# Routed experts: up part with standing weights and pieces of 256, 320 or 384 tokens

## The reference

```python
xn = _layernorm(x, axis=-1)
s = _L0_attn_ref(xn, W1, b1, W2, b2, init_h)          # recurrence, (.., 512) -> (.., 512)
# the expert part, on x = xn reshaped to (8192, 512); E = 32, I = 1024
shared_out = _swiglu(x, shared_gate_w, shared_up_w, shared_down_w)
logits = x @ gate_w
topk_ids = jnp.argmax(logits, axis=-1)
scores = jax.nn.sigmoid(jnp.max(logits, axis=-1))[:, None]
order = jnp.argsort(topk_ids)
sorted_x = (x * scores)[order]
g = ragged_dot(sorted_x, routed_gate_w, tokens_per_expert)   # (32, 512, 1024)
u = ragged_dot(sorted_x, routed_up_w, tokens_per_expert)     # (32, 512, 1024)
d = ragged_dot(silu(g) * u, routed_down_w, tokens_per_expert)  # (32, 1024, 512)
result = x_in + s * silu(shared_out + d[argsort(order)])
```

## Time and profile before

| what | value |
|---|---|
| runs | 4072.81, 4073.63, 4076.45 us; median 4073.63 |
| profiled execution | 4077.65 us, its span 4076.0 |
| TensorE busy | 3984.7 us, 98% |
| VectorE busy | 1983.8 us, 49% |
| ScalarE busy | 2003.6 us, 49% |
| mean granted clock of TensorE | 0.991 of 2.4 GHz |
| third sweep | from about 2607 us to the end, 4076 |

### The profile page before, as it was taken

The page is one execution under the profiler, slowest core; times in us unless marked ns, Lnnn a source line. Parts: engine busy times, 40 slices in busy tenths (PEclk is TensorE's granted clock), DMA queues, the critical chain, the costliest instruction groups (busy, mean ns, idle before and its releaser), DMA issues. The chain is left out here.

```text
span 4076.0 us, 51548 instructions
## 1 busy us (share of the span) xinstructions
PE 3984.7 (98%) x17849; PEld 3230.3 (79%) x17852; DVE 1983.8 (49%) x2711; ACT 2003.6 (49%) x2512; POOL 834.1 (20%) x927
## 2 busy tenths in 40 slices
PE   7999999999989999999999999799999999999998
PEld 6888888888867888888888888588888888888886
DVE  4232323233345555555555555455656556565564
ACT  3222222222247766766676666454545455554552
POOL 2011110101014100000000000043434434444443
PEclk9999999999989999999999999899999999999999
DMA  4122121212121000110000010455657557566562
GB/s 164 65 78 77 74 80 72 82 51 90 44 81 44 32 32 31 51 42 31 31 31 31 34 59 10 151 196 190 213 173 255 196 190 258 200 229 216 191 229 87
DMA packets 197850, 447.44 MB, mean 110 GB/s; under 512 B 19737, under 2 KB 36313, under 8 KB 193954
## 3 DMA queue, kind: packets, MB, share of 16 engines
q1 hardware_dynamic: 165170, 346.24, 24.0%
q0 software_dynamic: 32624, 100.47, 7.2%
HBM read 345.90 MB, written 104.68 MB: 111 GB/s over the span
## 5 line engine op out<-in xcount | busy, mean ns | idle before, releaser
L82 PE MATMUL gate<-xT,w_hi 128*128 128x512 f32 x1536 | 601.4, 392 | 1.1 <-DVE b2all L952 1.1
L83 PE MATMUL gate<-xT,w_hi 128*128 128x512 f32 x1536 | 601.4, 392 | 0.0
L84 PE MATMUL gate<-xT,w_lo 128*128 128x512 f32 x1536 | 599.6, 390 | 0.0
L1162 DVE TENSOR_TENSOR wlo<-raw,whi 128x2048 fp32r<-128x2048 f32 x192 | 438.7, 2285 | 83.5 <-ACT whi L1158 83.5
L1367 PE MATMUL tY<-whi,thT 128*128 128x512 f32 x1264 | 426.5, 408 | 0.0
L518 DVE TENSOR_TENSOR h_act<-h_act,psU 128x512 f32<-128x512 f32 x128 | 87.9, 687 | 685.8 <-PE psU L84 685.7
L1158 ACT ACTIVATE whi<-raw 128x2048 fp32r<-128x2048 f32 x192 | 367.3, 1913 | 42.1 <-DMA raw<-in_L_ffn_routed_gate_w 17.0
L82 PEld LDWEIGHTS gate<-xT,w_hi 128*128 128x128 f32 x1536 | 288.8, 188 | 66.2 <-DVE b2all L952 2.6
L84 PEld LDWEIGHTS gate<-xT,w_lo 128*128 128x128 f32 x1536 | 289.1, 188 | 62.1
L83 PEld LDWEIGHTS gate<-xT,w_hi 128*128 128x128 f32 x1536 | 288.8, 188 | 60.2
L966 DVE SCALAR_TENSOR_TENSOR log_f<-gate,b1s,log_f 128x512 f32<-128x512 f32 x128 | 96.2, 751 | 420.4 <-ACT log_f L893 420.4
(11 more groups left out here) (187 smaller groups left out, 8454.4 us busy)
## 6 DMA issues: line engine op xcount, KB each, us to landing
raw<-in_L_ffn_routed_gate_w SPq DMA_DIRECT2D x64, 1024.0 KB, 6.5
raw<-in_L_ffn_routed_up_w SPq DMA_DIRECT2D x64, 1024.0 KB, 6.3
raw<-in_L_ffn_routed_down_w SPq DMA_DIRECT2D x64, 1024.0 KB, 6.9
xT_dram<-xT SPq DMA_DIRECT2D x16, 2048.0 KB, 6.3
xT<-xT_dram SPq DMA_DIRECT2D x14, 2048.0 KB, 7.9
x_in<-in_L_attn_x SPq DMA_DIRECT2D x16, 1024.0 KB, 5.4
xs_dram<-x_in SPq DMA_DIRECT2D x16, 1024.0 KB, 4.4
ss_dram<-y_sb SPq DMA_DIRECT2D x64, 256.0 KB, 2.1
```

The costliest lines, as they stand in the source:

```text
L82: pe.matmul(out, w[0], x[0], start=start, stop=False)
L83: pe.matmul(out, w[0], x[1], start=False, stop=False)
L84: return pe.matmul(out, w[1], x[0], start=False, stop=stop)
L1162: dve.tensor_tensor(wlo[q][:], raw[q][:], whi[q][:], ALU.subtract).then_inc(wlo_done[q], 1)
```

## The change

The third sweep works on pieces instead of tiles. An expert's tokens are cut into full pieces of 384 (`PIECE`) and a last one, whose size is rounded up to 8, 10 or 12 units of 32 tokens: 256, 320 or 384. The sort is changed to give slots in units of 32 and a `plan` for each expert: first piece, first unit, first third group, number of full pieces, units of the last piece. VectorE writes in the recurrence sweep, for each piece, its expert and its size to `listed`.

In the up part the weights stand (128 inputs by 128 hidden channels) and the tokens of the piece stream, in 256, 320 or 384 columns. There are 16 blocks (gate and up for 8 groups of 128 hidden channels) of 12 matmuls. The result has hidden channels on the partitions, as the down part wants it, so `turn_h` is gone. The down part has 24 matmuls of 512 columns for each 128 tokens, into one of three psY banks; the third group is behind a condition. TensorE runs one loop over `listed`; only its up part has a program for each size. The other engines still loop over experts, with a full-piece program and one of three for the last piece. The raw weight buffers are three in a ring instead of six; each weight part is 1 MB as before, but a part of the up weights now holds 256 channels of gate and of up. Gathers are for three groups of 128 for each piece, whatever its size.

```diff
+UNIT = 32
+PIECE = 384
+SIZES = (8, 10, 12)
@@ recurrence_sweep, VectorE @@
-            dve.tensor_copy(starts[:], first_tile[0:1, :]).then_inc(starts_done, 1)
+            dve.tensor_copy(orders[:], plan[0:1]).then_inc(orders_done, 1)
+            def list_expert(e):
+                dve.scalar_tensor_tensor(piece_expert[:], numbers[:], plan[0:1, FIRST_PIECE, e:e + 1], piece_expert[:],
+                                         ALU.is_ge, ALU.add)
+                listing(dve.tensor_scalar(piece_this[:], numbers[:], last_place[:, e:e + 1], less[:, e:e + 1],
+                                          ALU.is_equal, ALU.mult))
+                listing(dve.tensor_tensor(piece_less[:], piece_less[:], piece_this[:], ALU.add))
@@ routed_sweep @@
-        raw = [k.sb(f"raw{q}", [P, 4, 512]) for q in range(PARTS)]
+        raw = [k.sb(f"raw{n}", [P, 4, 512]) for n in range(RING)]
+                p = order(eng, FIRST_PIECE, e, 0, E + MOST)
+                full = order(eng, FULL, e, 0, MOST)
+                n = order(eng, LAST, e, LEAST, MOST_UNITS)
+                with eng.If(full > 0):
+                    with eng.Fori(0, MOST) as i:
+                        with eng.If(full > i):
+                            piece(p + i, e, MOST_UNITS, False)
+                by_size(eng, n, lambda size: piece(p + full, e, size, split))
@@ SP @@
             with sp.Fori(1, E) as e:
                 for q in range(PARTS):
-                    sp.wait_ge(wlo_done[q], e)
-                    sp.dma_start(raw[q][:], part(q, e)).then_inc(raw_loaded[q], 16)
+                    if q < RING:
+                        sp.wait_ge(wlo_done[q + RING], e)
+                    else:
+                        sp.wait_ge(wlo_done[q - RING], e + 1)
+                    load_part(sp, q, e)
@@ ScalarE, a piece @@
+                for b in range(NI):
+                    silu(b)
+                    h_hi(b)
+                    if b % 2 == 1 and b < NI - 1:
+                        hi(b // 2)
+                act.wait_ge(u_mm, p * NI + NI)
+                x_hi(p + 1, 0)
+                hi(NQ - 1)
+                for g in range(1, GROUPS):
+                    x_hi(p + 1, g)
                 hi(D0)
+                for g, rows in groups(n):
+                    act.wait_ge(z_done[g], p + 2)
+                    act.activation(yo[g][0:rows], yo[g][0:rows], ACT.Silu).then_inc(zs_done[g], 1)
                 hi(D1)
@@ VectorE, a piece @@
+                for b in range(NI):
+                    h_mul(b)
+                    h_lo(b)
+                    if b % 2 == 1 and b < NI - 1:
+                        lo(b // 2)
+                x_lo(p + 1, 0)
+                lo(NQ - 1)
+                for g in range(1, GROUPS):
+                    x_lo(p + 1, g)
+                for g, rows in groups(n):
+                    total(g, rows)
+                    if g == 0:
+                        lo(D0)
+                    result(g, rows)
                 lo(D1)
@@ TensorE @@
+            def up_part(p, e, n):
+                N = n * UNIT
+                def up(b, m, bank, done):
+                    q, cols = b // 2, slice(b % 2 * P, b % 2 * P + P)
                     for kb in range(KD):
+                        mm = matmul_pairs(pe, bank[b % 2][:, 0:N],
+                                          [pair(w[q][:])[:, m, kb, cols] for w in (whi, wlo)],
+                                          [xT[:, a, kb, 0:N] for a in range(2)], kb == 0, kb == KD - 1)
+                    mm.then_inc(done, 1)
+                for b in range(NI):
+                    if b % 2 == 0:
+                        pe.wait_ge(wlo_done[b // 2], e + 1)
+                    pe.wait_ge(sg_done, p * NI + b + 1)
+                    up(b, 0, psG, g_mm)
+                    pe.wait_ge(h_done, p * NI + b + 1)
+                    up(b, 1, psU, u_mm)
+            with pe.Fori(0, E + MOST) as p:
+                with pe.If(total > p):
+                    e = pe.value_load(listed[0:1, 0, bass.ds(p, 1)], min_val=0, max_val=E - 1)
+                    n = pe.value_load(listed[0:1, 1, bass.ds(p, 1)], min_val=LEAST, max_val=MOST_UNITS)
+                    pe.wait_ge(xlo, (p + 1) * GROUPS)
+                    by_size(pe, n, lambda size: up_part(p, e, size))
+                    turn_x(p + 1, 0)
+                    pe.wait_ge(wlo_done[D0], e + 1)
+                    pe.wait_ge(hlo, p * NI + KH)
+                    pe.wait_ge(z_done[0], p + 1)
+                    down(0, 0)
+                    turn_x(p + 1, 1)
+                    pe.wait_ge(z_done[1], p + 1)
+                    down(0, 1).then_inc(d0_mm, 1)
+                    turn_x(p + 1, 2)
+                    pe.wait_ge(z_done[2], p + 1)
+                    third(n, 0, d0_mm)
+                    pe.wait_ge(wlo_done[D1], e + 1)
+                    pe.wait_ge(hlo, p * NI + NI)
+                    for g in range(2):
+                        down(1, g).then_inc(y_mm[g], 1)
+                    third(n, 1, y_mm[2])
```

More of the change, by code:

```diff
@@ new lines, in routed_sweep, with order, unit, by_size @@
+        out_stored = [k.sem(f"out_stored{g}") for g in range(GROUPS)]
+        block = ctx.enter_context(nc.Block())
+        def order(eng, what, e, least, most):
+            return eng.value_load(orders[0:1, what, bass.ds(e, 1)], min_val=least, max_val=most)
+        def unit(u):
+            return nc.s_assert_within(u, 0, NU, skip_runtime_bounds_check_because="the units of all experts are NU at most")
+        def by_size(eng, n, body, sizes=SIZES):
+            if len(sizes) == 1:
+                return body(sizes[0])
+            half = len(sizes) // 2
+            with eng.If(n > sizes[half - 1]):
+                by_size(eng, n, body, sizes[half:])
+            with eng.Else():
+                by_size(eng, n, body, sizes[:half])
@@ L1258, in tile @@
+                if len(groups(n)) < GROUPS:
+                    act.sem_inc(zs_done[2], 1)
                 hi(D1)
-            experts(act, tile)
+            experts(act, piece)
         @block.vector
         def _(dve):
-            for n in range(2):
-                dve.sem_inc(h_done[n], 1)
-                dve.sem_inc(hlo[n], 1)
-            dve.sem_inc(z_done, 1)
-            dve.sem_inc(zm_done, 1)
-            def x_lo(t):
-                dve.wait_ge(xhi, t + 1)
-                dve.tensor_tensor(xT[:, 1], psX[:], xT[:, 0], ALU.subtract).then_inc(xlo, 1)
@@ L1275, in _, with x_lo @@
-            dve.wait_ge(returned, 16)
-            dve.tensor_copy(back[:], back_i[:]).then_inc(back_done, 1)
+            dve.sem_inc(h_done, 2)
+            for g in range(GROUPS):
+                dve.sem_inc(z_done[g], 1)
+            def x_lo(p, g):
+                dve.wait_ge(xhi, p * GROUPS + g + 1)
+                dve.tensor_tensor(xT[:, 1, :, turned(g)], psX[:], xT[:, 0, :, turned(g)], ALU.subtract).then_inc(xlo, 1)
+            by_step = [t[:, 0:NU].rearrange("p (s n) -> p n s", n=STEP) for t in (scatter_at, gather_at)]
@@ new lines, in down, with third @@
+            def down(half, g):
+                q = D0 + half
+                for kb in range(KH):
+                    b = half * KH + kb
+                    for a, w in ((0, whi), (0, wlo), (1, whi)):
+                        mm = pe.matmul(psY[g][:], hT[:, a, b, g * P:(g + 1) * P], w[q][:, kb, :],
+                                       start=b == 0 and a == 0 and w is whi, stop=b == NI - 1 and a == 1)
+                return mm
+            def third(n, half, done):
+                with pe.If(n > 2 * STEP):
+                    down(half, 2).then_inc(done, 1)
+                with pe.Else():
+                    pe.sem_inc(done, 1)
```

552 lines of the change are left out of this document (313 added, 239 removed).

## The result

| | us |
|---|---|
| before | 4074.84 median (4072.81 to 4076.45, 4 runs) |
| after | 4322.34 median (4318.26 to 4330.81, 4 runs) |
| ratio | 1.061, 95% interval 1.0592 to 1.0629 |
| profiled execution after | span 4329.1, mean granted clock 0.956 (before 0.991) |

The change costs 6.1%, 247 us; I had forecast a gain of 1.1%. First the page after, which answers to the earlier trace rows: TensorE is busy for 40 us less in all, and stands for 293 us more (385 against 91). In its line of the clock, each digit the granted clock of a fortieth of the span, the third sweep (the last 16 digits) now begins at 7 and later swings between 8 and 9.

The account below looks back on a forecast made before the run. The prediction took TensorE's matmul issue to bound the routed part wholly. Span 4076.0 - 49.6 for that part + 5 for small parts = 4031.4 us, given as 4029 us against the median, range 4012 to 4050.

Parts of the forecast that it names:

- the switch: TensorE between pieces: register loads, choice of program and conditional thirds take 1.3 us a piece, bounds 0.3 and 4.
- The table load in front of Silu (1.28) fits beside that: ScalarE at a piece's start: its 1.28 us table load runs beside VectorE's way to the first h at 9.54.
- Rival C: TensorE stalls jumping into a size's program, switch 5 us instead of 1.3; 4120 us, slower; 13%.
- the dearer of the two values: Up part matmuls: 14 us per thousand fixed on each, so 0.120, 0.147, 0.173 us; 825 us in sum, not 790.
- rival D: Up part: weight loads take their record's 0.19 us, so every up matmul does; 300 us more, 4330; 4%.
- TensorE's own time for a piece: TensorE's work for a piece, switch included: 36.8 us at 256 tokens, 47.4 at 320, 52.5 at 384.
- The chain: In-order weight splits and hidden-state steps on ScalarE and VectorE hold 256 pieces at 38.4 us, not 36.8.
- 320 pieces are hidden: At 320 tokens, two groups' splits and steps take 6.4 us against TensorE's 7.06, so they don't hold it.
- The start: Start of the routed part: second piece begins at 2675.7 instead of tile 3 at 2668.63; bounds 3 us better, 6 worse.
- The sort's cost: The plan adds some 14 VectorE steps in the sort's last chunk, 3 us beside TensorE's matmuls; +3 taken with the list.
- The list: Six steps in each of 16 recurrence units, about 1.2 us, covered by VectorE's 3.3 us waits; uncovered, up to 20 us.
- the prologue: Loads and splits before the first piece: gathers and table move them by 6 us, the ring's waits by 0.5 net.

Follow-up runs that it names:

- e1: The changed kernel with the never-taken program for full pieces removed from ScalarE's expert loop, 232 instructions left; 4084.98 us, ratio 1.002.
- e9: e1 with each wlo one place later on VectorE, which also loses the program for full pieces; 4020.79 us, ratio 0.9864.
- e3: e1 with lagged wlo, ScalarE's whi of D1 moved behind the next piece's first two groups, VectorE also without full pieces; 4005.35 us, ratio 0.9822.

## Why the prediction was wrong, step by step

**The step that failed: what a change of piece costs was asked of TensorE only.** The prediction priced the switch on TensorE (1.3 us, bounds 0.3 and 4), and for ScalarE it says "The table load in front of Silu (1.28) fits beside that". Nothing was charged for ScalarE's jump back, its register loads and its choice. Measured, they are some 3.4 + 2.7 + 3.6 us, of which whi of D1 covers under 2, in front of the table load. TensorE's waits on it are 253.9 us in the changed kernel and 27.1 in e1. The windows from the second piece to the last matmul, of e1 and then of the changed kernel, add the clock: for the same 8151 matmuls TensorE is busy 47 us longer, 1.6 us a piece.

```profile
2700.00:4064.00 1364.00, 1289.21 (x8151) 1181.43 (x8150) 835.38 (x1000) 653.55 (x876) 556.56 (x448) 1.00 0.65 221
```

```profile
2704.00:4310.00 1606.00, 1335.97 (x8151) 1236.01 (x8150) 838.77 (x998) 655.71 (x876) 468.10 (x448) 0.91 0.57 189
```

With 25 us less in front of tX (38.0 in this window of e1, 12.5 here) that makes 248; the stretch from the second piece to the end of the last matmul is 1610.4 - 1368.0 = 242 us longer.

**Rival C** (13%) had the mechanism, a jump into a size's program that stalls, but on the wrong engine. It looked at TensorE because the three programs of 384 instructions stand there, and its evidence against (expert starts cost 0.50 - 0.23 on TensorE) says nothing about ScalarE. Its price, 4120, came from 5 us on TensorE; on ScalarE there are 10 us, and behind them a slower clock, which no rival had. The diff did show what mattered: three programs for the last piece and one for full pieces, on every engine that loops over experts. Counting the instructions of each loop would have shown 84 become 298. That this is too much stands in no row of before; yet the earlier trace rows has ScalarE at the head of the expert's loop with a table load, just where a delay has the least slack.

**Right, with numbers.** Pieces: 32, as 17, 13 and 2. Matmul spacing: 0.120, 0.147 and 0.173 us, the dearer of the two values, as in the rows at 3138.72 and 3138.83 and in the loads below. The Trainium skill's "TensorE: Matmul & The Clock Gate", section "Back-to-back issue gap", gives N/2.4 + 2.5 ns for an isolated gap, 109 ns at 256 columns. In this stream of matmuls, each with its own weight load, that is 10 to 11 ns short at each width, and the trace decides. Weight loads (rival D): loads of 0.19 us start with the matmuls, 0.12 apart, and hold nothing back:

```profile
3138.83 0.19 PEld L89 LDWEIGHTS tG<-txT,wlo 128*128 128x128 f32 x1
3138.95 0.19 PEld L87 LDWEIGHTS tG<-txT,whi 128*128 128x128 f32 x1
```

TensorE's own time for a piece: right to 0.2 us without the 1.3 for the switch, which is nought. Steps of 256 columns: 0.42 measured for the rounded copy (0.38 taken), 0.38 for Silu, 0.42 on VectorE.

**The chain was right in kind, mis-sized at one end.** 38.4 us was forecast, 40.5 measured in e1. For a steady 256 piece of e1 TensorE's stops are 2.0 us in front of tX (forecast 1.9) and 0.4 and 0.3 within the rounds (forecast 0.3 each, 6.1 against 5.76), but also 1.6 us in front of the third group, for which I had nothing. TensorE, then ScalarE, at that place of e1:

```profile
3118.73 0.39 PE L87 MATMUL tG<-txT,whi 128*128 128x256 f32 x1 [1.43 <-ACT tsg L1415]
```

```profile
3114.42 1.90 ACT L1291 ACTIVATE whi<-raw 128x2048 fp32r<-128x2048 f32 x1
3117.00 1.28 ACT L1415 ACT_TABLE_LOAD   x1 [0.68 <-issue]
3118.30 0.38 ACT L1415 ACTIVATE tsg<-tG 128x256 f32<-128x256 f32 x1
```

The table load does not fit beside anything: it stands behind whi of D1 and in front of the Silu that TensorE waits for, even where nothing stalls. e9 keeps this stop and loses the others, e3 moves whi of D1 and loses most of it. That 320 pieces are hidden failed with it, 47.2 against their own 45.9; that 47.2 lies so near the forecast 47.4 is luck, as 1.3 us of stops stand where 1.3 us of switch were charged. The 33.7 us are thus the 256 pieces (some 37 us over 16 of them, TensorE's first entries included), less some 3 on the others.

**The start was mis-sized in three places.** The sort's cost does not show: the recurrence's first `log_f` on VectorE starts at 1185.73 before and at 1186.37 in e1, and over all the profiled executions at 1184.3 to 1187.2 with the old sort and at 1183.6 to 1190.4 with the new one. From there to the last copy of the state on POOL it takes 1410.9 us in each of the six kernels with the recurrence of before, and 1419.9 or 1421.5 in the seven with the list. The last copy, before and in e1:

```profile
2596.62 0.18 POOL L846 COPY state<-hs 128x1 f32<-128x1 f32 x1 [10.83 <-DVE hs L927]
```

```profile
2606.27 0.19 POOL L884 COPY state<-hs 128x1 f32<-128x1 f32 x1 [10.71 <-DVE hs L965]
```

That is 9.7 us later, of which I had charged 3. The list is the only thing added there, and waits of 3.3 us a unit didn't cover it: argued from where it appears, not tested. The second place is the prologue. The last whi ended 38.3 us behind that copy before; I had added 6.5, and in e1 it ends 50.9 us behind it, 6.2 more. The loads of D0 and D1 wait in the ring for wlo of parts 1 and 2, the last at 2647.44; I had charged the wait for wlo but not the load's own 8 us behind it:

```profile
2644.01 4.34 SPq L1267 DMA_DIRECT2D raw<-in_L_ffn_routed_down_w  x4
```

```profile
2655.30 1.91 ACT L1291 ACTIVATE whi<-raw 128x2048 fp32r<-128x2048 f32 x1 [4.05 <-DMA raw<-in_L_ffn_routed_down_w]
2662.53 1.28 ACT L1415 ACT_TABLE_LOAD   x1 [5.32 <-issue]
```

The third place is the second of these rows: from the end of the last whi to the third group of channels 7.1 us pass, where I had 1.7. ScalarE's first entry into a program of the sweep takes 4.6 us, though its loop is short in e1. The last 1.4 us of the 19.6 were not taken apart.

## What to carry to other kernels

Where a change gives an engine several programs in a loop, count the instructions of that loop on every engine, also of branches that never run, and look at what stands first behind the loop's head. A jump or a choice is priced on the engine with the least slack at that moment, not on the one whose work changes. When two in-order engines pass work to and fro, a wlo that follows its whi at once makes every later step of the round wait; one place later, as in e9, the stops within the rounds were gone.

## What the runs showed of the hardware

- ScalarE (231 and 264 instructions) and VectorE (267) run their loop at 0.2 to 0.3 us a jump. With 286, 298 and 352 on ScalarE and 406 on VectorE two jumps in each turn, the one back and the one over a program or a dead branch, cost 2.4 to 6.5 us each, with some 5 instruction packets of 8 KB a turn. In the kernel before 22 dead instructions cost 340 us (286 was run once). Even with 298, a step to the program right behind the choice (384) took 0.1 us, and the jump over the 58 instructions in front of the choice 0.2 us. Where a loop begins in the program was not varied on ScalarE.
- TensorE's loop of 721 instructions shows no such stall once the sweep runs; early entries cost 9.1 and 3.1 us, and 2.3 to 4.6 in front of the third piece, the first of 320 tokens. ScalarE's first entry costs 4.6 us, in a loop of 232 as well (e1).
- A stop of 8 us dropped the granted clock to its lower level: 0.52 in the window behind it, starts 0.21 us apart at 256 columns instead of 0.12, for about 4 us.
